# Row selection moved to ScalarE, and four more turns of the rank blocks moved to VectorE

## The chip, the cores and the metric

The kernel runs on one core of a Trainium2 chip. The metric is the device time of one execution in microseconds. Three executions of the kernel before took 880.44, 880.70 and 880.80 us (median 880.7).

## The reference, cut to what matters

Two layers are applied to 4096 tokens of width 1024, and each adds its result to its input.

```python
x = x + _L0_ffn_ref(_L0_cond_ref(x, ...), W_base, b_base, W_router, A, B)
x = x + _L1_ffn_ref(_L1_cond_ref(x, weight, bias, lora_a_weights, lora_b_weights,
                                 scaling_factors, adapter_id), base_W, router_W, lora_A, lora_B)
# L0_ffn: router logits, top 2 of 8 experts, softmax over the two, rank 16 per expert
logits = xf @ W_router.T
rw, sel = jax.lax.top_k(logits, TOP_K)
rw = jax.nn.softmax(rw, axis=-1)
h = jnp.einsum('td,erd->ter', xf, A)
lora = jnp.einsum('ter,te,eor->to', h, w, B) * SCALING
# L1_cond: one of 8 adapters of rank 16 for every sequence of 64 tokens
a_sel = lora_a_weights[adapter_id]
b_sel = lora_b_weights[adapter_id]
low = jnp.einsum('bsi,bri->bsr', x, a_sel)
delta = jnp.einsum('bsr,bor->bso', low, b_sel)
# L1_ffn: router, top 2 of 8, rank 16 per expert, as in L0_ffn
```

The kernel multiplies the weights of both layers together once (about the first 350 us). What is left for each token is one large product with the combined matrix, the router logits, and three low-rank parts: the rank block `m0` (8 experts x 16 = 128 columns) of the first layer, the adapter's low rank `low` of the second, and the rank block `mid` of the second layer.

## The kernel before, in words

After the weights, 16 tiles of 256 tokens are worked through (tiles 0 to 15, `tau`). Tiles 0 and 1 use plain products (`plain_products`, 96 matmuls of 128x512 each), tiles 2 to 15 a Winograd scheme with fewer matmuls (`winograd_products`). Every fp32 factor is split into a high part, written by ScalarE (`hi_of`, L1143), and a low part, written by VectorE (`lo_of`, L1516); a product is three matmuls.

The engines each run an own list, written out by hand, and meet at semaphores. For a tile the small chain is this, in order of data:

- TensorE: `x_product(tau)` multiplies the tile by `gx`, which holds the logits' and ranks' columns and, at two places for each block `b` of 128 tokens, the 16 columns of the adapter that the sequence has chosen. TensorE waits for `gsel_ok` there.
- VectorE: `front(tau)` (`route`, L1962 to L1985) takes the top two experts, and L1994 multiplies the ranks by their weights: `m0`. In the middle it needs an exponential from ScalarE (`rex`, L1398).
- `m0` is turned (tokens to ranks) into bank `TR`: in tiles 0 and 1 by TensorE, with two 128x128 transposes (`turn`, L856); from tile 2 on by VectorE (`m0_turn`, L2039), with 16 block transposes of 32x64.
- ScalarE: `m0_high`; VectorE: `m0_low`; TensorE: step x1 of `chain(tau, i)` (L871 to L873), which adds the turned `m0` times its columns. `i` counts the matmuls of the tile, and the table `CHAIN` says at which `i` TensorE stops for a step of the chain: (turn of m0, x1, mid) by tile.
- VectorE: `low_rank` (L2008, needs `gx`'s partner `bls`), `low_low`; TensorE: step mid of the chain (L884); VectorE: `back(tau)`, the second routing, whose product L2031 is `mid`.
- `mid` is turned: in tiles 0, 1, 2 and 15 by TensorE (`mid_turn`), in tiles 3 to 14 by VectorE. `mid_high`, `mid_low`; then the rank products of TensorE (L1114 to L1116 in tiles 0 and 1, L923 later).

Who chooses the adapter's columns: GpSimd. Its loop waits for `c_mm` and `lraw_s` of the tile before, loads an index from memory to a register four times (`value_load`), and after each copies 16 elements into `bls` (L577) and 18x16 into `gx` (L578). Only then does it wait for `c2_mm` and issue the tile's `p1sel` DMAs (L566).

Between these steps VectorE and ScalarE make the other factors: in tiles 0 and 1 the sums and splits `t2_raw`, `t4_raw`, `t1_raw` (L2069 to L2083) and `t_high`/`t_low`, whose results SyncE stores and loads again; the split of the next tile (`x_high`, `x_low`); and the copies of the four output banks (`out_copy`, L1423), which free a bank for the next tile (`ev[j]`). TensorE begins a tile's bank 0 after `ev[0]`. In Winograd tiles VectorE adds partial results (`out_parts`, L2162), and TensorE waits for the first of these sums, `x6_ok`, before it uses bank 4 again; and for `u3_part` (L2171) before the last low term.

Of the kernel before, what the change touches and what calls it, by code (L numbers as in the profile page):

```python
# [14 lines left out]
P = 128  # L15
# [4 lines left out]
E = 8  # L20
# [14 lines left out]
KH = KC // 2  # L35
CHAIN = [(30, 44, 76), (13, 24, 56), (None, 29, 46), (None, 29, 46)]
R7, R6, R4, R2, R3, R5, NR = 1, 2, 3, 4, 5, 6, 6
# [34 lines left out]
def build(nc, xq, wall, m1t, aallt, x0t, b0t, lb1, lorabt, loraa, wq, cbook, ids, packed, out,  # L72
          e_dram, p1_dram, b_dram, t_dram):
    with ExitStack() as ctx:
# [439 lines left out]
        def _(pool):  # L514
# [54 lines left out]
            for tau in range(NT2):  # L569
                if tau:  # L570
                    pool.wait_ge(c_mm, tau)
                    pool.wait_ge(lraw_s, tau)
                for b, c0 in enumerate((0, WX)):
                    for s in range(2):
                        n = tau * 4 + 2 * b + s
                        i = bass.ds(pool.value_load(idc[0:1, n:n + 1], min_val=0, max_val=E - 1), 1)
                        nc.gpsimd.tensor_copy(bls[:, b, s, :], bl[:, i, :].squeeze(1))  # L577
                        ins = nc.gpsimd.tensor_copy(gx[:, :, c0 + RK * s:c0 + RK * s + RK], gl[:, i, :, :].squeeze(1))  # L578
                ins.then_inc(gsel_ok, 1)
                if tau:  # L580
                    pool.wait_ge(c2_mm, tau)
                else:
                    pool.wait_ge(gsel_ok, 1)
                    pool.wait_ge(g_mm, M_ALL)
                    nc.gpsimd.memset(f(lowt[96:KL, :]), 1.0).then_inc(pz_ok, 1)
                    pool.wait_ge(pz_ok, 1)
                    nc.gpsimd.memset(f(lowt[96:96 + RK, :]), 0.0).then_inc(pz_ok, 1)
                    pool.wait_ge(pz_ok, 2)
                    for b in range(2):
                        nc.gpsimd.memset(f(p1sel[b][32:64, :]), 0.0).then_inc(pz_ok, 1)  # L590
                    pool.wait_ge(pz_ok, 4)
                load_p1(tau, ld_p1s, slice(D, NM1))
                if tau:
                    pool.wait_ge(low_mm, tau)
                load_p1(tau, ld_p1w, slice(0, D))
# [3 lines left out]
        def _(pe):  # L599
# [240 lines left out]
            def x_product(tau, halves=(0, 1)):  # L840

                u, last = tau if tau < REG else 0, KH * halves[-1] + KH
                pe.wait_ge(x_hi_s, 2 * tau + halves[-1] + 1)
                pe.wait_ge(x_lo_s, 2 * tau + halves[-1] + 1)
                pe.wait_ge(gsel_ok, tau + 1)
                for b in range(2):
                    cs, ts = slice(SX * b, SX * b + WX), slice(b * P, b * P + P)
                    for c in range(KH * halves[0], last):
                        mm = split_product(xb[:, b, cs], x_hi[u][:, c, ts], x_lo[u][:, c, ts],
                                           gx[:, c, cs], gx[:, 9 + c, cs], c == 0, c == KC - 1)  # L850
                if last == KC:
                    mm.then_inc(xx_mm, 1)

            def turn(v, n0):
                for b in range(2):
                    mm = nc.tensor.transpose(TR[:, n0 + b * P:n0 + b * P + P], v[:, b, :], ident)  # L856
                return mm

            def chain(tau, i):
                at_m0, at_x1, at_mid = CHAIN[min(tau, REG) + (tau + 1 == NT2)]  # L860
                if i == at_m0:
                    pe.wait_ge(m0_s, tau + 1)
                    turn(m0, 0).then_inc(t0_mm, 1)
                if i == at_x1:
# [23 lines left out]
            def mid_turn(tau):  # L888
                pe.wait_ge(mid_s, tau + 1)
                turn(midv, 0).then_inc(t2_mm, 1)  # L890

# [34 lines left out]
            def winograd_products(tau):  # L926
# [74 lines left out]

                if n:
                    pe.wait_ge(mid_s, tau + 1)
                else:
                    mid_turn(tau)
                x_product(tau + 1, (0,))
# [113 lines left out]
            low_terms(0, (0, 2, 1, 3))  # L1120
            mid_turn(0)
            x_product(1)
# [17 lines left out]
        def _(act):  # L1140
# [135 lines left out]
            hi_of(brow[0][0:1, 512:D], bk[6][0:1, :]).then_inc(brow_hi, 1)  # L1276

            def x_hi_part(tau, k):
                cs = slice(KH * k, KH * k + KH)
# [67 lines left out]
            x_hi_part(0, 0).then_inc(x_hi_s, 1)  # L1347
            x_hi_part(0, 1).then_inc(x_hi_s, 1)
            act.wait_ge(eb_lo_s, 14)
            for q in range(4):  # L1350
# [83 lines left out]
            x_high(1, 1)  # L1434
            t_high(1)
            rex(0, 1)
            mid_high(0)
            t_high(2)
            for j in (3, 0, 2, 1):
                out_copy(0, j)  # L1440
            rex(1, 0)
            x_high(2, 0)
            m0_high(1)
            x_high(2, 1)
            low_stack(1)
            t_high(3)
            rex(1, 1)
            mid_high(1)
            s_high(2, 1)
# [10 lines left out]
            for tau in range(REG, NT2):  # L1460
# [18 lines left out]
                if tau + 1 < NT2:  # L1479
                    x_high(tau + 1, 0)  # L1480
                rex(tau, 1)
                if tau + 1 < NT2:
                    x_high(tau + 1, 1)
                mid_high(tau)
# [20 lines left out]
        def _(v):  # L1505
# [494 lines left out]
            def low_rank(tau):  # L2000
                v.wait_ge(c_mm, tau + 1)
                v.wait_ge(gsel_ok, tau + 1)
                twice = lambda a: a.unsqueeze(1).to_broadcast([64, 2, RK])
# [38 lines left out]
            def m0_turn(tau):  # L2042
                v.wait_ge(m0_s, tau + 1)
                turn(m0).then_inc(t0_mm, 1)

# [30 lines left out]

            def t1_raw(h, between=None):
                r, (h12, l12), (h11, l11) = t_begin(3, h), g_part(h, 0, 1), g_part(h, 0, 0)
                link(nc.vector.tensor_tensor(r, h12, h11, ALU.subtract))
                if between:  # L2080
                    between()
                link(nc.vector.tensor_tensor(r, r, l12, ALU.add))
                nc.vector.tensor_tensor(r, r, l11, ALU.subtract).then_inc(t_raw_s, 1)  # L2083

            def t_low(n):
                for h in range(2):
                    cs = slice(2 * h, 2 * h + 2)
# [99 lines left out]

            v.wait_ge(gsel_ok, 1)
            link(nc.vector.memset(shares[:], 1.0))
            front(0)  # L2190
            v.wait_ge(af_hi_s, 4)
            lo_of(lb1_lo[:], lb1_raw[:], lb1_hi[:]).then_inc(af_lo_s, 1)
            v.wait_ge(af_lo_s, 4)
            t_low(0)
            m0_low(0)
            t2_raw(0)
# [5 lines left out]
            t_low(1)  # L2202
            back(0)
            t4_raw(0)
            t4_raw(1)
            mid_low(0)
            t_low(2)
            front(1)
            x_low(2, 0)
            m0_low(1)  # L2210
            x_low(2, 1)
            t1_raw(0, lambda: low_rank(1))
            low_low(1)
            t1_raw(1)
# [10 lines left out]
            for tau in range(REG, NT2):  # L2225
# [26 lines left out]
                back(tau, lambda: s3_low(tau))  # L2252
                if n and tau + 1 < NT2:
                    mid_turn(tau)
# [98 lines left out]
```

## Time and profile before

| | us |
|---|---|
| median of three executions | 880.7 |
| the profiled execution | 881.12 |
| its span | 878.9 |
| TensorE busy | 873.8 |
| VectorE busy | 768.1 |
| ScalarE busy | 325.8 |
| GpSimd busy | 157.1 |

The span is the part of the execution in which instructions run, 2.2 us less than its time. The granted clock of TensorE is full in all slices of the span but the last. Busy time of TensorE counts overlapping matmuls once. Times in rows are microseconds from the span's start. Tile 0 begins at 345 us, tile 1's large products at 388, tile 2's at 425; from tile 3 on a tile takes 32.6 us.

### The profile page before, as it was taken

The page shows a single profiled execution, that of the slowest core. Times are in us where ns is not written, and L with a number is a line of the kernel's source. Part 1 is how long each engine was busy: PE and PEld are TensorE (multiplying, and loading weights), DVE is VectorE, ACT ScalarE, POOL GpSimd, SP SyncE. Part 2 cuts the span into 40 slices and gives each one's busy share as a digit, 9 for nine tenths or more (in the row PEclk, how much of TensorE's full clock was granted, in tenths as well). Part 3 has the DMA queues.
Part 4 walks back from the last instruction along what each step waited for, and adds up shares of the span by engine and source line. Part 5 has one row for each costly group of instructions (what it writes and reads, how often), then busy time and mean ns, then how long its engine had stood idle before and what let it go on. Part 6 is the DMA issues. An engine that isn't in the chain of part 4 may idle for free.

```text
span 878.9 us, 13788 instructions
## 1 busy us (share of the span) xinstructions
PE 873.8 (99%) x4506; PEld 766.8 (87%) x4506; DVE 768.1 (87%) x1846; ACT 325.8 (37%) x525; POOL 157.1 (18%) x310
## 2 busy tenths in 40 slices
PE   9999999999999999999999999999999999999998
PEld 8999998888998888888888888888888888888887
DVE  6899999787787968878889999999999999999995
ACT  6589788421424434232322222222223223222221
POOL 0210020111001001412212312312312312302310
PEclk9999999999999999999999999999999999999999
DMA  9623440685412042484887987987887988887976
GB/s 346 224 93 118 126 138 25 212 273 177 143 49 96 1 144 75 152 312 174 251 273 265 313 291 256 307 298 257 301 294 256 307 277 275 305 287 257 314 253 224
DMA packets 62610, 191.93 MB, mean 218 GB/s; under 512 B 8256, under 2 KB 12742, under 8 KB 60620
## 3 DMA queue, kind: packets, MB, share of 16 engines
q1 hardware_dynamic: 50282, 158.92, 51.6%
q0 software_dynamic: 11968, 31.88, 12.8%
q8 instruction: 36, 0.59, 0.3%
q10 hardware_dynamic: 290, 0.26, 0.1%
q14 instruction: 34, 0.28, 0.1%
HBM read 158.80 MB, written 32.76 MB: 218 GB/s over the span
## 4 chain that ended last, share of the span: by engine, by line
PE 97%; DMA 2%; ACT 0%; DVE 0%; SPq 0%; issue 0%; DVEq 0%
PE bank L941 16%; PE bank L603 15%; PE bank L604 15%; PE bank L605 15%; PE bank L965 9%; PE bank L923 7%; PE bank L909 5%; PE bank L969 4%; PE bank L640 2%; PE bank L918 2%; PE bank L1066 2%; PE bank L747 2%; DMA t_lo<-t_scratch 1%; PE bank L647 1%; DMA m_raw<-m1t 0%; PE bank L618 0%
## 5 line engine op out<-in xcount | busy, mean ns | idle before, releaser
L941 PE MATMUL bank<-g_hi,xs 128*128 128x512 f32 x440 | 140.1, 390 | 0.0
L566 POOL DMA_DIRECT2D p1sel<-p_scratch x128 | 65.6, 512 | 263.6 <-issue 263.4
L2039 DVE STREAM_TRANSPOSE bank<-ranks_raw 32x64 f32<-32x64 f32 x416 | 106.5, 256 | 6.2
L941 PEld LDWEIGHTS bank<-g_hi,xs 128*128 128x128 f32 x440 | 82.6, 188 | 17.1
L965 PE MATMUL bank<-t_hi,xs 128*128 128x512 f32 x336 | 91.1, 393 | 0.0
L941 PE MATMUL bank<-g_lo,xs 128*128 128x512 f32 x220 | 86.5, 393 | 0.0
L603 PE MATMUL bank<-gx,xs 128*128 128x304 f32 x256 | 77.6, 303 | 0.0
L605 PE MATMUL bank<-gx,xs 128*128 128x304 f32 x256 | 77.4, 303 | 0.0
L604 PE MATMUL bank<-gx,xs 128*128 128x304 f32 x256 | 77.1, 301 | 0.0
L965 PEld LDWEIGHTS bank<-t_hi,xs 128*128 128x128 f32 x336 | 63.0, 188 | 14.3 <-DMA t_hi<-t_scratch 0.2
L1516 DVE TENSOR_TENSOR xs<-x_raw,xs 128x1024 fp32r<-128x1024 f32 x60 | 73.6, 1249 | 2.1 <-ACT xs L1143 1.2
L1143 ACT ACTIVATE xs<-x_raw 128x1024 fp32r<-128x1024 f32 x60 | 61.6, 1050 | 25.5 <-PE bank L969 24.7
L577 POOL COPY bls<-bl 128x16 f32 x64 | 33.9, 529 | 170.1 <-issue 84.9
L1695 DVE SCALAR_TENSOR_TENSOR rbuf<-qbuf,thr,rbuf 128x1024 f32<-128x1024 f32 x48 | 59.5, 1281 | 3.5 <-ACT rbuf L1202 3.0
L1202 ACT ACTIVATE rbuf<-rbuf,step 128x1024 f32<-128x1024 f32 x48 | 53.8, 1148 | 9.3 <-DVE rbuf L1689 6.2
L604 PE MATMUL bank<-m_lo,w_hi 128*128 128x388 f32 (+1 forms) x168 | 56.9, 338 | 0.0
L603 PE MATMUL bank<-m_hi,w_hi 128*128 128x388 f32 (+1 forms) x168 | 56.9, 338 | 0.0
L605 PE MATMUL bank<-m_hi,w_lo 128*128 128x388 f32 (+1 forms) x168 | 56.8, 338 | 0.0
L969 PE MATMUL bank<-t_lo,xs 128*128 128x512 f32 x168 | 51.9, 390 | 0.1
L605 PE MATMUL bank<-weff_hi,w_lo 128*128 128x512 f32 x128 | 49.8, 389 | 0.0
L604 PE MATMUL bank<-weff_lo,w_hi 128*128 128x512 f32 x128 | 49.8, 389 | 0.0
L603 PE MATMUL bank<-weff_hi,w_hi 128*128 128x512 f32 x128 | 49.8, 389 | 0.0
(390 smaller groups left out, 2122.3 us busy)
## 6 DMA issues: line engine op xcount, KB each, us to landing
t_hi<-t_scratch SPq DMA_DIRECT2D x82, 512.0 KB, 5.7
t_lo<-t_scratch SPq DMA_DIRECT2D x82, 512.0 KB, 6.7
x_raw<-xq SPq DMA_DIRECT2D x16, 1024.0 KB, 6.8
out<-ost SPq DMA_DIRECT2D x63, 256.0 KB, 6.6
p1sel<-p_scratch POOLq DMA_DIRECT2D x64, 192.0 KB, 6.0
w_raw<-wall SPq DMA_DIRECT2D x15, 512.0 KB, 4.8
w<-e_scratch SPq DMA_DIRECT2D x6, 1024.0 KB, 5.2
ea<-e_scratch POOLq DMA_DIRECT2D x8, 644.0 KB, 5.3
```

Of the source, the lines that this page charges most:

```text
L566: pool.dma_start(f(p1sel[b][64 * s:64 * s + STK, cs]), p1_dram[bass.ds(i * STK, STK), cs]).then_inc(sems[b], 16)
L603: nc.tensor.matmul(out_ap, lhs_hi, rhs_hi, start=first, stop=False, skip_group_check=True)
L604: nc.tensor.matmul(out_ap, lhs_hi, rhs_lo, start=False, stop=False, skip_group_check=True)
L605: return nc.tensor.matmul(out_ap, lhs_lo, rhs_hi, start=False, stop=last, skip_group_check=True)
L923: mm = nc.tensor.matmul(dst, l, m, start=first and k == 0, stop=k == 2, skip_group_check=True)
L941: mm = nc.tensor.matmul(bk[j][:], l[:, c, :], m[:, c, :], start=first and c + k == 0, stop=c + k == KH + 1, skip_group_check=True)
L965: nc.tensor.matmul(bk[j][:], x[u][:, c, :], t_hi[:, c, :], start=first and c + u == 0, stop=False, skip_group_check=True)
L969: mm = nc.tensor.matmul(bk[j][:], x[0][:, c, :], t_lo[:, c, :], start=False, stop=c == KH - 1, skip_group_check=True)
L1143: return nc.scalar.activation(dst, src, ACT.Identity)
L1516: return nc.vector.tensor_tensor(dst, src, f(hi), ALU.subtract)
L1695: nc.vector.scalar_tensor_tensor(rbuf[u][:], qbuf[u][:], thr[:, m:m + 1], rbuf[u][:], ALU.is_gt, ALU.mult).then_inc(r_ready[u], 1)
L2039: ins = nc.vector.transpose(turned[ks, :, ts], ranked[ts, :, ks])
```

## The change

ScalarE copies the adapter's columns (`select`), in two halves for each tile, each with its own place in ScalarE's list; `gsel_ok` now counts two for each tile, and who waits for it waits for both. GpSimd keeps only the DMAs. VectorE now turns `m0` of tiles 0 and 1 and `mid` of tiles 0 and 2, with its 16 block transposes, and TensorE keeps the turn of `mid` in tiles 1 and 15. The lists of VectorE and ScalarE in tiles 0 and 1 are put in another order around this, and `CHAIN` loses its first column and has other places for x1 and mid: x1 of tile 0 goes from matmul 44 to 39, x1 of tile 1 from 24 to 28, mid of tile 1 from 56 to 57.

```diff
-CHAIN = [(30, 44, 76), (13, 24, 56), (None, 29, 46), (None, 29, 46)]
+CHAIN = [(39, 76), (28, 57), (29, 46), (29, 46)]
...                                                    # GpSimd
             for tau in range(NT2):
                 if tau:
-                    pool.wait_ge(c_mm, tau)
-                    pool.wait_ge(lraw_s, tau)
-                for b, c0 in enumerate((0, WX)):
-                    for s in range(2):
-                        n = tau * 4 + 2 * b + s
-                        i = bass.ds(pool.value_load(idc[0:1, n:n + 1], min_val=0, max_val=E - 1), 1)
-                        nc.gpsimd.tensor_copy(bls[:, b, s, :], bl[:, i, :].squeeze(1))
-                        ins = nc.gpsimd.tensor_copy(gx[:, :, c0 + RK * s:c0 + RK * s + RK], gl[:, i, :, :].squeeze(1))
-                ins.then_inc(gsel_ok, 1)
-                if tau:
                     pool.wait_ge(c2_mm, tau)
...                                                    # TensorE, x_product
-                pe.wait_ge(gsel_ok, tau + 1)
+                pe.wait_ge(gsel_ok, 2 * tau + 2)
...                                                    # TensorE, chain
-                if i == at_m0:
-                    pe.wait_ge(m0_s, tau + 1)
-                    turn(m0, 0).then_inc(t0_mm, 1)
...                                                    # TensorE, tile 2 (n == 0) and tile 0
-                if n:
-                    pe.wait_ge(mid_s, tau + 1)
-                else:
-                    mid_turn(tau)
+                pe.wait_ge(mid_s, tau + 1)
...
-            mid_turn(0)
+            pe.wait_ge(mid_s, 1)
             x_product(1)
...                                                    # ScalarE
+            def select(tau, b):
+                c0 = WX * b
+                if tau:
+                    act.wait_ge(c_mm, tau)
+                    act.wait_ge(lraw_s, tau)
...
+                for s in range(2):
+                    n = tau * 4 + 2 * b + s
+                    i = bass.ds(act.value_load(idc[0:1, n:n + 1], min_val=0, max_val=E - 1), 1)
+                    nc.scalar.activation(bls[:, b, s, :], bl[:, i, :].squeeze(1), ACT.Identity)
+                    ins = nc.scalar.activation(gx[:, :, c0 + RK * s:c0 + RK * s + RK], f(gl[:, i, :, :].squeeze(1)),
+                                               ACT.Identity)
+                ins.then_inc(gsel_ok, 1)
...                                                    # ScalarE, before the tiles
             x_hi_part(0, 1).then_inc(x_hi_s, 1)
+            select(0, 0)
+            select(0, 1)
...                                                    # ScalarE, tiles 0 and 1
             t_high(1)
+            select(1, 0)
             rex(0, 1)
+            select(1, 1)
             mid_high(0)
             t_high(2)
-            for j in (3, 0, 2, 1):
+            for j in (3, 0):
                 out_copy(0, j)
             rex(1, 0)
+            for j in (2, 1):
+                out_copy(0, j)
             x_high(2, 0)
...                                                    # ScalarE, tiles 2 to 15
                     x_high(tau + 1, 0)
+                    select(tau + 1, 0)
                 rex(tau, 1)
                 if tau + 1 < NT2:
+                    select(tau + 1, 1)
                     x_high(tau + 1, 1)
...                                                    # VectorE
             front(0)
+            m0_turn(0)
...
+            m0_low(0)
             t_low(0)
-            m0_low(0)
             t2_raw(0)
...
             back(0)
+            mid_turn(0)
             t4_raw(0)
+            mid_low(0)
             t4_raw(1)
-            mid_low(0)
-            t_low(2)
+            t_low(2, (0,))
             front(1)
+            m0_turn(1)
+            m0_low(1)
+            t_low(2, (1,))
+            low_rank(1)
             x_low(2, 0)
-            m0_low(1)
+            low_low(1)
             x_low(2, 1)
-            t1_raw(0, lambda: low_rank(1))
-            low_low(1)
+            t1_raw(0)
             t1_raw(1)
...
-                if n and tau + 1 < NT2:
+                if tau + 1 < NT2:
                     mid_turn(tau)
```

VectorE's list in tile 0, from the product of the second routing (`ranks_raw<-bank,gate`, which is `mid`) to the first routing of tile 1 (`MAX`). Before:

```order
L2031 TENSOR_TENSOR ranks_raw<-bank,gate 128x256
L2074 TENSOR_TENSOR t_raw<-g_hi,t_raw 128x1024
L2075 TENSOR_TENSOR t_raw<-t_raw,g_lo 128x1024
L2074 TENSOR_TENSOR t_raw<-g_hi,t_raw 128x1024
L2075 TENSOR_TENSOR t_raw<-t_raw,g_lo 128x1024
L1516 TENSOR_TENSOR midt_lo<-bank,midt_hi 128x256
L1516 TENSOR_TENSOR t_lo<-t_raw,t_hi 128x1024 x2
L1962 MAX best<-bank 128x8
```

The same place of the changed kernel:

```order
L2038 TENSOR_TENSOR ranks_raw<-bank,gate 128x256
L2046 STREAM_TRANSPOSE bank<-ranks_raw 32x2x32 x16
L2083 TENSOR_TENSOR t_raw<-g_hi,t_raw 128x1024
L2084 TENSOR_TENSOR t_raw<-t_raw,g_lo 128x1024
L1523 TENSOR_TENSOR midt_lo<-bank,midt_hi 128x256
L2083 TENSOR_TENSOR t_raw<-g_hi,t_raw 128x1024
L2084 TENSOR_TENSOR t_raw<-t_raw,g_lo 128x1024
L1523 TENSOR_TENSOR t_lo<-t_raw,t_hi 128x1024
L1969 MAX best<-bank 128x8
```

The 16 block transposes and `mid_low` now stand ahead of the second half of `t4_raw`, and one of the two instructions of `t_low(2)` has gone behind the routing.

ScalarE's list over the same time, from `mid_high(0)` to the first split of tile 2. Names `ost_84`, `ost_81`, `ost_83`, `ost_82` are the output copies of banks 3, 0, 2, 1. Before:

```order
L1143 ACTIVATE midt_hi<-bank 128x256
L1143 ACTIVATE t_hi<-t_raw 128x1024 x2
L1423 ACTIVATE ost_84<-bank 128x512
L1423 ACTIVATE ost_81<-bank 128x512
L1423 ACTIVATE ost_83<-bank 128x512
L1423 ACTIVATE ost_82<-bank 128x512
L1398 ACTIVATE shares<-shares 128x2
L1143 ACTIVATE xs<-x_raw 128x4x256
```

The changed kernel, from the last index of `select(1, 1)` on:

```order
L1269 TENSOR_LOAD idc
L1269 ISA x2
L1270 ISA
L1270 ACTIVATE bls<-bl 128x16
L1271 ISA
L1271 ACTIVATE gx<-gl 128x18x16
L1123 ACTIVATE midt_hi<-bank 128x256
L1123 ACTIVATE t_hi<-t_raw 128x1024 x2
L1422 ACTIVATE ost_84<-bank 128x512
L1422 ACTIVATE ost_81<-bank 128x512
L1397 ACTIVATE shares<-shares 128x2
L1422 ACTIVATE ost_83<-bank 128x512
```

The exponential of tile 1's first routing now comes after two output copies, not four; the output copies still stand behind both halves of `t_hi`.

## Rows read from the trace of the kernel before

**Rows 1.** The page, busy time of each engine.
```profile
PE 873.8 (99%) x4506; PEld 766.8 (87%) x4506; DVE 768.1 (87%) x1846; ACT 325.8 (37%) x525; POOL 157.1 (18%) x310
```

**Rows 2.** TensorE's longest wait in the span: engine, line, releaser: us, times, longest.
```profile
PE bank L629 <- DVE warm L1560: 1.1, 1, 1.1
```

**Rows 3.** Timeline of TensorE, m0's turn in tile 0: start, duration, instruction.
```profile
358.65 0.38 PE L856 MATMUL bank<-pk,ranks_raw 128*128 128x128 f32 x2
358.79 0.48 PE L909 MATMUL bank<-g_hi,xs 128*128 128x512 f32 x1
359.10 0.40 PE L909 MATMUL bank<-g_lo,xs 128*128 128x512 f32 x1
```

**Rows 4.** Timeline of VectorE, m0's turn in blocks in tile 2.
```profile
424.48 0.42 DVE L1994 TENSOR_TENSOR ranks_raw<-bank,gate 128x256 f32<-128x256 f32 x1
424.94 4.30 DVE L2039 STREAM_TRANSPOSE bank<-ranks_raw 32x64 f32<-32x64 f32 x16
429.69 0.42 DVE L1516 TENSOR_TENSOR m0t_lo<-bank,m0t_hi 128x256 fp32r<-128x256 f32 x1 [0.45 <-ACT m0t_hi L1143]
```

**Rows 5.** Timeline of VectorE, tile 0; in brackets idle time before, and its releaser.
```profile
359.49 0.42 DVE L1516 TENSOR_TENSOR m0t_lo<-bank,m0t_hi 128x256 fp32r<-128x256 f32 x1 [1.59 <-ACT m0t_hi L1143]
...
362.98 0.59 DVE L2008 TENSOR_TENSOR lraw<-bank,bls 64x32 f32<-64x32 f32 x4 [0.68 <-PE bank L873]
...
379.20 1.23 DVE L2075 TENSOR_TENSOR t_raw<-t_raw,g_lo 128x1024 f32<-128x1024 f32 x1
```

**Rows 6.** Timeline of TensorE: mid's turn of tile 0, and tile 1's first large product.
```profile
378.60 0.38 PE L856 MATMUL bank<-pk,ranks_raw 128*128 128x128 f32 x2
...
388.26 0.39 PE L909 MATMUL bank<-g_hi,xs 128*128 128x512 f32 x1
```

**Rows 7.** Timeline of ScalarE: the output copies, then a split and an exponential in tile 3.
```profile
386.40 2.65 ACT L1423 ACTIVATE ost<-bank 128x512 f32<-128x512 f32 x4 [2.94 <-PE bank L1116]
...
467.40 1.05 ACT L1143 ACTIVATE xs<-x_raw 128x1024 fp32r<-128x1024 f32 x1
471.20 0.20 ACT L1398 ACTIVATE shares<-shares 128x2 f32<-128x2 f32 x1 [2.75 <-DVE shares L1965]
```

**Rows 8.** Timeline of VectorE, tile 1.
```profile
385.71 0.18 DVE L1962 MAX8 best<-bank 128x8 f32<-128x8 f32 x1 [0.98 <-PE bank L605]
...
389.18 0.17 DVE L1977 TENSOR_SCALAR rs<-shares 128x2 f32<-128x2 f32 x1 [2.30 <-ACT shares L1398]
...
392.05 0.42 DVE L1516 TENSOR_TENSOR m0t_lo<-bank,m0t_hi 128x256 fp32r<-128x256 f32 x1 [0.61 <-ACT m0t_hi L1143]
...
415.88 0.42 DVE L1516 TENSOR_TENSOR midt_lo<-bank,midt_hi 128x256 fp32r<-128x256 f32 x1 [1.55 <-ACT midt_hi L1143]
...
422.15 0.17 DVE L1962 MAX8 best<-bank 128x8 f32<-128x8 f32 x1 [0.18 <-PE bank L605]
```

**Rows 9.** Timeline of VectorE, tile 2 and the start of tile 3.
```profile
432.16 0.59 DVE L2008 TENSOR_TENSOR lraw<-bank,bls 64x32 f32<-64x32 f32 x4 [0.72 <-PE bank L873]
...
436.33 1.47 DVE L1516 TENSOR_TENSOR xs<-x_raw,xs 128x1024 fp32r<-128x1024 f32 x1
...
450.64 0.69 DVE L2171 TENSOR_TENSOR p_sum<-bank,p_sum 128x512 f32<-128x512 f32 x1 [1.73 <-PE bank L923]
...
453.98 0.17 DVE L1962 MAX8 best<-bank 128x8 f32<-128x8 f32 x1 [0.39 <-PE bank L605]
...
463.14 0.42 DVE L1516 TENSOR_TENSOR m0t_lo<-bank,m0t_hi 128x256 fp32r<-128x256 f32 x1
```

**Rows 10.** Timeline of TensorE, tile 3: step x1, and the product that needs the selection.
```profile
464.12 0.29 PE L871 MATMUL bank<-gx,m0t_hi 128*128 128x272 f32 x1
...
475.55 0.30 PE L603 MATMUL bank<-gx,xs 128*128 128x304 f32 x1
```

**Rows 11.** Timeline of GpSimd, tile 3: two of the four copies into bls.
```profile
466.38 0.20 POOL L577 COPY bls<-bl 128x16 f32 x1 [6.94 <-DVE lraw L2008]
...
467.17 0.58 POOL L577 COPY bls<-bl 128x16 f32 x1 [0.22 <-issue]
```

More of the change, by code:

```diff
@@ L570, in _ @@
                 if tau:
-                    pool.wait_ge(c_mm, tau)
-                    pool.wait_ge(lraw_s, tau)
-                for b, c0 in enumerate((0, WX)):
-                    for s in range(2):
-                        n = tau * 4 + 2 * b + s
-                        i = bass.ds(pool.value_load(idc[0:1, n:n + 1], min_val=0, max_val=E - 1), 1)
-                        nc.gpsimd.tensor_copy(bls[:, b, s, :], bl[:, i, :].squeeze(1))
-                        ins = nc.gpsimd.tensor_copy(gx[:, :, c0 + RK * s:c0 + RK * s + RK], gl[:, i, :, :].squeeze(1))
-                ins.then_inc(gsel_ok, 1)
-                if tau:
                     pool.wait_ge(c2_mm, tau)
                 else:
-                    pool.wait_ge(gsel_ok, 1)
                     pool.wait_ge(g_mm, M_ALL)
@@ L852, in x_product @@
                     mm.then_inc(xx_mm, 1)
[L854 to L857, printed above, removed]
             def chain(tau, i):
-                at_m0, at_x1, at_mid = CHAIN[min(tau, REG) + (tau + 1 == NT2)]
-                if i == at_m0:
-                    pe.wait_ge(m0_s, tau + 1)
-                    turn(m0, 0).then_inc(t0_mm, 1)
+                at_x1, at_mid = CHAIN[min(tau, REG) + (tau + 1 == NT2)]
                 if i == at_x1:
@@ L889, in mid_turn @@
                 pe.wait_ge(mid_s, tau + 1)
-                turn(midv, 0).then_inc(t2_mm, 1)
+                for b in range(2):
+                    mm = nc.tensor.transpose(TR[:, b * P:b * P + P], midv[:, b, :], ident)
+                mm.then_inc(t2_mm, 1)
             def plain_products(tau):
@@ L1276, in _ @@
             hi_of(brow[0][0:1, 512:D], bk[6][0:1, :]).then_inc(brow_hi, 1)
+            def select(tau, b):
[3 more added lines that the diff above has]
+                    act.wait_ge(lraw_s, tau)
+                elif not b:
+                    act.wait_ge(ids_ok, 2)
+                    act.wait_ge(g_lo_s, OC11)
+                    act.wait_ge(bias_ok, 1)
+                for s in range(2):
[5 more added lines that the diff above has]
+                ins.then_inc(gsel_ok, 1)
             def x_hi_part(tau, k):
@@ L1445, in _ @@
             low_stack(1)
+            select(2, 0)
             t_high(3)
             rex(1, 1)
+            select(2, 1)
             mid_high(1)
@@ L2001, in low_rank @@
                 v.wait_ge(c_mm, tau + 1)
-                v.wait_ge(gsel_ok, tau + 1)
+                v.wait_ge(gsel_ok, 2 * tau + 2)
                 twice = lambda a: a.unsqueeze(1).to_broadcast([64, 2, RK])
@@ L2043, in m0_turn @@
                 v.wait_ge(m0_s, tau + 1)
+                if not tau:
+                    v.wait_ge(g_lo_s, O_ALL)
                 turn(m0).then_inc(t0_mm, 1)
@@ L2075, in t4_raw, with t1_raw, t_low @@
                 nc.vector.tensor_tensor(r, r, l21, ALU.add).then_inc(t_raw_s, 1)
-            def t1_raw(h, between=None):
+            def t1_raw(h):
                 r, (h12, l12), (h11, l11) = t_begin(3, h), g_part(h, 0, 1), g_part(h, 0, 0)
                 link(nc.vector.tensor_tensor(r, h12, h11, ALU.subtract))
-                if between:
-                    between()
                 link(nc.vector.tensor_tensor(r, r, l12, ALU.add))
                 nc.vector.tensor_tensor(r, r, l11, ALU.subtract).then_inc(t_raw_s, 1)
-            def t_low(n):
-                for h in range(2):
+            def t_low(n, parts=(0, 1)):
+                for h in parts:
                     cs = slice(2 * h, 2 * h + 2)
@@ L2186, in out_lower_right @@
                 out_sum(tau, 3, bk[4], p1_sum)
-            v.wait_ge(gsel_ok, 1)
+            v.wait_ge(gsel_ok, 2)
             link(nc.vector.memset(shares[:], 1.0))
             front(0)
+            m0_turn(0)
             v.wait_ge(af_hi_s, 4)
```

## The prediction, made before the changed kernel had run

> **What bounds the kernel now.** I read the page first: TensorE is busy 873.8 of 878.9 us, VectorE 768.1, ScalarE 325.8, GpSimd 157.1 [rows 1]. Then TensorE's waits: the longest is 1.1 us, at the very start [rows 2], and nothing in the tiles names VectorE or ScalarE. So TensorE is the bound, and time can be won only by taking work from it. Last I read the timelines of the first tiles, because the change works there, and ask of every step how long before TensorE's need it is done. The answer is: seldom more than 1 us. The profiled execution took 881.12 us, its span 878.9; the median of the runs is 0.42 lower, 880.7. I add to 881.12 and take the 0.42 off at the end.
>
> **What TensorE is relieved of.** A pair of transposes starts at 358.65, where the next large matmul would have started. The second large matmul after that point starts at 359.10 [rows 3]; two large matmuls in a row start 0.23 apart (358.65 to 358.88), so a pair delays TensorE by 0.22. Four pairs go (m0 and mid of tile 0, m0 of tile 1, mid of tile 2): 4 x 0.22 = 0.88 us. Those of tiles 1 (mid) and 15 stay. That is all the gain TensorE can show: 881.12 - 0.88 = 880.24 if nothing is late.
>
> **What VectorE is given.** A turn in blocks takes 4.30 and begins 0.46 after the product before it (424.48 to 424.94), where an instruction that needs nothing would have begun after some 0.35: 4.4 us each, four times 17.6. A split that follows a turn directly also waits 0.45 for ScalarE [rows 4]. A rule of the Trainium skill speaks against such a move (VectorE: DVE Perf Modes, Rules for kernel authors): transpose 128x128 with TensorE if the result may go to PSUM, as it does here. By the trace the rule's prices are 0.22 against 4.30 us. By busy time alone the move would be worth its 0.88 us; by the rule it is bad wherever VectorE is what TensorE waits for next. So I follow VectorE through three places.
>
> **First place: the output bank that tile 1 begins with.** Before, VectorE ended `t4_raw(1)` at 379.20 + 1.23 = 380.43. Added ahead of that: two turns, 8.8, and `mid_low`, 0.4. What this fills: the waits of 1.59 and 0.68 in tile 0 [rows 5], and about 0.5 that the copies of GpSimd cost VectorE and that end (a split which takes 1.23 elsewhere took 1.47 beside them in tile 2 [rows 9]; I take twice the difference for a tile, an estimate). 380.43 + 9.2 - 2.77 = 386.9. Then ScalarE has the second half of `t_hi` (1.05, by the like split of rows 7) and two output copies (2.65 / 4 = 0.66 each, and a little less as no matmul holds them back): `ev[0]` at 389.0 to 389.2. TensorE would be there at 388.26 [rows 6] less two pairs, 387.8. So a wait of about 1.2 us, and more than the whole gain is gone. Before, the copies ended at 389.05 all four, and bank 0's was long done [rows 7]; now `t_hi`'s second half comes before them. Step x1 of tile 0 (matmul 39, nine matmuls of 0.23 after 358.65, 360.7) is just met: adding VectorE's list from its first routing gives `m0t_lo` at 360.4.
>
> **Second place: step x1 of tile 1 and the start of tile 2.** The routing of tile 1 begins at 386.9 + 1.1 = 388.0, 2.3 later than 385.71. To the routing of tile 2: + 4.4 + 0.45 (turn and its split), + 1.2 (the other half of `t_low(2)`); filled are waits of 2.30, 0.61 and 1.55, and two more of about half a us each, like the 0.61 [rows 8]; GpSimd gives back 0.5 to 0.8. VectorE was ready for tile 2 at 421.97. 421.97 + 2.3 + 6.05 - 4.46 - 1.0 - 0.65 = 424.2; adding the instructions of this stretch in their new order by their spacing gives 423.6, so 1.4 to 2.0 late. TensorE meets x1 of tile 1 about when m0t_lo is ready (395.4), so it waits at most 0.2 there, and in tile 2 it had 1.2 us to spare at x1 (m0t_lo done at 430.1 [rows 4]; `low_rank`, which starts some 0.9 after x1 does, at 432.16 [rows 9]); VectorE is late by 1.4 or more, TensorE itself by 0.5: no wait, or one of a few tenths.
>
> **Third place: step x1 of tile 3.** Before, `m0t_lo` was done at 463.14 + 0.42 = 463.56 and TensorE took it at 464.12 [rows 9, 10]. Now VectorE comes 1.5 late, has mid's turn (4.4), and can fill 0.72, 1.73 and 0.39 [rows 9] and 0.5 from GpSimd: 463.56 + 1.5 + 4.4 - 2.84 - 0.5 = 466.1. On the way TensorE waits twice, for `u3_part` (about 0.1) and for `x6_ok`, the first sum of `out_parts`, some 1.0. Whatever was waited for before is part of this one: TensorE's x1 goes from 464.12 to 466.1 or 466.2. **The sum is +2.0 us**: 0.88 won, 2.9 waited (about 1.2 at `ev[0]`, 0.1 at x1 of tile 1, 1.1 in tile 2's end, 0.5 at x1 of tile 3). From tile 3 on VectorE does what it did, without GpSimd's copies beside it, and TensorE's own pace returns. 881.12 + 2.0 = 883.1; less 0.42: 882.7.
>
> **The selection on ScalarE.** GpSimd came to its next index after 0.79 us (466.38 to 467.17) while the copies went on [rows 11]. On ScalarE no row shows a load of an index. Low end: the same 0.79, so a half of two indices takes 1.6 and the last copy 0.4: 2.0. High end: the load not hidden behind the two copies, which by 0.20 for 2 elements and 1.05 for 1024 [rows 7] take 0.2 and 0.45: 1.43 an index, 2.9 a half. In tile 3 ScalarE is free from 468.4 to 471.2 and again from 471.4 until TensorE needs the columns at 475.55 [rows 7, 10]: 2.8 and 4.1. For tile 1 the second half begins behind the exponential, at about 375.5 by VectorE's new list, and TensorE comes at 378.60 - 0.22 [rows 6]: 2.9. Both ends fit; I take nothing. If a half took over 3.5, the two halves and the exponential would pass 475.55 in each of 13 tiles. The Trainium skill gives a floor of about 600 ns for a tensor_load (DMA: Bandwidth & Descriptors, Latency and other measured facts); by it an index would cost some 0.3 more than GpSimd's, an estimate, still inside the high end. The DMAs of GpSimd come 1 to 2 us sooner, as they no longer stand behind the copies; nobody waits for them, so nothing.
>
> **Rivals.**
> A, the forecast: VectorE is late by its turns, +2.0, own range +0.8 to +3.4. For it: VectorE has 2.8 us of idle time in tile 2 to set against 4.4, and three hand-overs with under 1 us to spare.
> B, not slower: the turns are hidden, because VectorE gains more from the end of GpSimd's copies and from the new order than I count. It must be 2.9 us earlier at x1 of tile 3 for the full gain, 2.0 for no change: 880.7 - 0.9 = 879.8 in full, up to 880.7 + 0.8 in part. For it: all three places are sums of many short terms, and each was off by a few tenths when I added it in two ways. Against it: 17.6 us of turns, and the idle spans named at the three places add up to 10.6 (2.27 + 4.46 + 1.0 + 2.84).
> C, the selection: a half takes 3.5 + h us on ScalarE and TensorE waits 2h in each of 13 tiles; with h of 0.2 that is 5 us, 887. Against it: the bounds above. It decides from 3.5 on.
> D, VectorE doesn't recover: the lateness of tile 3 returns at x1 in later tiles, as it had only 0.5 to spare; 0.3 in each of 5 tiles, 884.5.
>
> **How the numbers follow.** A 0.60, B 0.24, C 0.07, D 0.09. The predicted time is A's, 882.7. The range 880.0 to 885.0 leaves out the full B's lower part, C, and the far end of D, and holds about 8 in 10. 0.2% is 1.76 us and about what a measurement here can tell: slower than 882.46 are six tenths of A, C and D: 0.52. Same is the rest of A and most of B: 0.43. Faster than 878.9 would need twice what the four pairs cost: 0.05.
>
> **What the profile would show.** Right: TensorE has waits that name ScalarE's output copy L1422 at about 388 (1 us), VectorE's L2169 (`out_parts`) at about 457 (1 us) and `m0t_lo` at about 465; VectorE has 480 block transposes of bank, not 416; its splits beside the old copies fall from 1.47 to 1.23; from tile 4 on no waits. Wrong: no TensorE wait between 350 and 470 (B), or waits on `gx` in each tile with ScalarE's L1271 as releaser (C), or at x1 in tile after tile (D).

## The result and the profile after

The changed kernel took 881.77 us (median of 22 executions, 881.62 to 882.88), the kernel before 880.72 beside it (22 executions, 880.12 to 882.27). The ratio is 1.0013, 95% interval 1.0007 to 1.0019: slower by 1.05 us, which is less than the 0.2% named as what counts. The forecast was 882.7, range 880.0 to 885.0. The profiled execution took 882.67, its span 881.0 us.

The page's busy times, to set against [rows 1]:

```profile
PE 874.2 (99%) x4498; PEld 766.5 (87%) x4498; DVE 773.9 (88%) x1910; ACT 358.9 (41%) x653; POOL 96.5 (11%) x182
```

The four pairs of transposes are gone (8 matmuls fewer), yet TensorE is not less busy. VectorE has 5.8 us more, less than the 17.6 that it was given. Three groups of the view by line show the most of why, first of the changed kernel, then of the kernel before (line, form, count | busy us, mean ns):

```profile
L2046 DVE STREAM_TRANSPOSE bank<-ranks_raw 32x64 f32<-32x64 f32 x480 | 122.9, 256 | 7.2
L1523 DVE TENSOR_TENSOR xs<-x_raw,xs 128x1024 fp32r<-128x1024 f32 x60 | 72.0, 1222 | 2.5 <-ACT xs L1123 2.1
L1523 DVE TENSOR_TENSOR lowt<-lowr,lowt 16x128 fp32r<-16x128 f32 x32 | 9.0, 283 | 1.3 <-ACT lowt L1123 0.6
```

```profile
L2039 DVE STREAM_TRANSPOSE bank<-ranks_raw 32x64 f32<-32x64 f32 x416 | 106.5, 256 | 6.2
L1516 DVE TENSOR_TENSOR xs<-x_raw,xs 128x1024 fp32r<-128x1024 f32 x60 | 73.6, 1249 | 2.1 <-ACT xs L1143 1.2
L1516 DVE TENSOR_TENSOR lowt<-lowr,lowt 16x128 fp32r<-16x128 f32 x32 | 14.7, 460 | 1.3 <-ACT lowt L1143 0.6
```

64 more block transposes, 16.4 us, as expected. The splits of the tiles, whose mean was 1249 ns beside GpSimd's copies, are at 1222 without them, 1.6 us less in all. The larger part comes from the small subtraction in `low_low`: 32 instructions, 5.7 us less.

TensorE's waits of 0.2 us or more (line, releaser: us, times, longest). Of these, before had only the first [rows 2]:

```profile
PE bank L592 <- ACT gx L1271: 1.4, 1, 1.4
PE bank L618 <- DVE warm L1567: 1.1, 1, 1.1
PE bank L906 <- DVE p_sum L2169: 0.6, 1, 0.6
PE bank L852 <- DVE m0t_lo L1523: 0.2, 1, 0.2
PE bank L952 <- DMA t_lo<-t_scratch: 0.2, 1, 0.2
```

The view counts a wait from the modelled end of the matmul before. What TensorE loses is read better from the starts, which are 0.23 apart for two 128x512 matmuls. TensorE's timeline at the three places:

```profile
378.15 0.40 PE L1046 MATMUL bank<-p1sel,lowt 114*128 114x512 f32 x1
379.93 0.38 PE L592 MATMUL bank<-gx,xs 128*128 128x304 f32 x1 [1.38 <-ACT gx L1271]
...
457.24 0.39 PE L906 MATMUL bank<-lb_hi,srk_lo 128*128 128x512 f32 x1
458.23 0.50 PE L906 MATMUL bank<-k_hi,srk_hi 128*128 128x512 f32 x1 [0.61 <-DVE p_sum L2169]
458.57 0.39 PE L906 MATMUL bank<-k_lo,srk_hi 128*128 128x512 f32 x1
...
465.38 0.39 PE L924 MATMUL bank<-g_lo,xs 128*128 128x512 f32 x1
465.95 0.36 PE L852 MATMUL bank<-gx,m0t_hi 128*128 128x272 f32 x1 [0.18 <-DVE m0t_lo L1523]
```

Ahead of tile 1 it loses 1.78 - 0.23 = 1.55 us, at `x6_ok` 0.99 - 0.23 and another 0.10 (0.34 to the next start), 0.9 in all, and at x1 of tile 3 0.57 - 0.23 and a tenth behind it, 0.4. With 0.88 won that is 2.0, and x1 of tile 3 starts at 465.95, 1.83 after that of before [rows 10]. There was no wait at the output bank of tile 1. In its place stands the one that the prediction had set at nothing, for the columns that ScalarE chooses. ScalarE's timeline there:

```profile
375.38 0.20 ACT L1397 ACTIVATE shares<-shares 128x2 f32<-128x2 f32 x1 [3.03 <-DVE shares L1972]
377.53 0.22 ACT L1270 ACTIVATE bls<-bl 128x16 f32 x1 [1.95 <-issue]
377.65 0.43 ACT L1271 ACTIVATE gx<-gl 128x288 fp32r x1
379.24 0.22 ACT L1270 ACTIVATE bls<-bl 128x16 f32 x1 [1.16 <-issue]
379.36 0.43 ACT L1271 ACTIVATE gx<-gl 128x288 fp32r x1
```

"issue" means that the engine waited for no semaphore: it was loading the index. The instructions of that line, over the whole span and then from 370 to 374 us (durations in ns, min/median/max):

```profile
L1269 ACTq TENSOR_LOAD <-idc x64: 272/277/1741, 323.4 to 832.8; - x64
...
L1269 ACTq TENSOR_LOAD <-idc x2: 275/278/282, 370.4 to 371.2; - x2
```

The longest of them, 1.74 us, begins at 375.44, as soon as the exponential has started.

GpSimd has index loads too, one for each `p1sel` DMA (L565). In the trace of the kernel before, where ScalarE loads no index, three of them fall in this stretch and take about 1 us or more, against a median of 289 ns:

```profile
L565 POOLq TENSOR_LOAD <-idc x3: 996/1217/1503, 373.1 to 378.8; - x3
```

So the sign of a slow stretch stood in the trace that the prediction was made from.

### The profile page after: what moved, and what is told of

It reads as the page before. It is cut to its first block, busy times and chain, and to the rows that moved or that the text cites. A ratio compares the mean times of both kernels' runs of the same rounds, so it can differ in the third digit from the quotient of the medians.

```text
span 881.0 us, 13856 instructions
## 1 busy us (share of the span) xinstructions
PE 874.2 (99%) x4498; PEld 766.5 (87%) x4498; DVE 773.9 (88%) x1910; ACT 358.9 (41%) x653; POOL 96.5 (11%) x182
## 4 chain that ended last, share of the span: by engine, by line
PE 90%; DVE 6%; DMA 2%; issue 1%; ACT 0%; ACTq 0%; SPq 0%; DVEq 0%
PE bank L924 15%; PE bank L592 15%; PE bank L594 15%; PE bank L593 15%; PE bank L948 8%; PE bank L906 6%; PE bank L952 4%; PE bank L892 2%; PE bank L629 2%; PE bank L736 2%; PE bank L1046 1%; DMA t_lo<-t_scratch 1%; DVE bank L2046 1%; PE bank L901 1%; PE bank L636 1%; DVE xs L1523 1%
## 5 line engine op out<-in xcount | busy, mean ns | idle before, releaser
L2046 DVE STREAM_TRANSPOSE bank<-ranks_raw 32x64 f32<-32x64 f32 x480 | 122.9, 256 | 7.2
L1523 DVE TENSOR_TENSOR xs<-x_raw,xs 128x1024 fp32r<-128x1024 f32 x60 | 72.0, 1222 | 2.5 <-ACT xs L1123 2.1
L592 PEld LDWEIGHTS bank<-gx,xs 128*128 128x128 f32 x256 | 48.2, 188 | 2.9 <-issue 1.8
```

The source lines that it names most:

```text
L592: nc.tensor.matmul(out_ap, lhs_hi, rhs_hi, start=first, stop=False, skip_group_check=True)
L1523: return nc.vector.tensor_tensor(dst, src, f(hi), ALU.subtract)
L2046: ins = nc.vector.transpose(turned[ks, :, ts], ranked[ts, :, ks])
```

## Experiments

Theory V: VectorE's list up to x1 of tile 3 decides the time, and the wait for `gx` lies beside it. Theory S: the wait for `gx` is the loss.

**The selection back on GpSimd.** On GpSimd the loop of the kernel before, with `ins.then_inc(gsel_ok, 2)`; on ScalarE:

```diff
-            select(1, 0)
             rex(0, 1)
-            select(1, 1)
...
-                    select(tau + 1, 0)
                 rex(tau, 1)
...
```

> The changed kernel with one part undone: GpSimd chooses the columns again, as before; the four turns stay on VectorE and every list else is that of the changed kernel. Theory V (VectorE's list up to step x1 of tile 3 sets the time, and TensorE's wait of 1.5 us for gx in front of tile 1 lies beside it): the wait for gx goes, a wait for the output copy of bank 0 of about 1.2 us takes its place at 388, VectorE's splits beside GpSimd's copies take some 1.4 us instead of 1.23 and x1 of tile 3 comes 0.3 to 1.0 us later than in the changed kernel: 882.0 to 882.8 us, against 881.8 of the changed kernel. Theory S (the wait for gx is the loss): it goes and nothing takes its place, 880.2 us.

Measured: 884.49 us (5 executions, from 883.93; ratio 1.0042, 1.0028 to 1.0056). Theory S has fallen, and theory V's size was too small. The page's busy times, then TensorE's waits from 345 us on:

```profile
PE 874.7 (99%) x4498; PEld 766.2 (87%) x4498; DVE 783.4 (89%) x1910; ACT 324.9 (37%) x525; POOL 159.3 (18%) x310
```

```profile
PE bank L903 <- ACT ost L1414: 1.4, 1, 1.4
PE bank L917 <- DVE p_sum L2155: 0.6, 1, 0.6
PE bank L959 <- ACT ost L1414: 0.4, 1, 0.4
PE bank L1057 <- DVE p_sum L2164: 0.3, 1, 0.3
```

The predicted wait for the output copy has appeared (L903, 1.4), and a second at the start of tile 2 (L959). VectorE is busy 9.5 us longer than in the changed kernel (783.4): GpSimd's copies cost it 0.6 us in each of 16 tiles. Three tiles of that are 1.8, and x1 of tile 3 is later by 1.9:

```profile
467.86 0.37 PE L863 MATMUL bank<-gx,m0t_hi 128*128 128x272 f32 x1
```

So without the move of the selection the turns would cost 2.7 us more by the medians, 1.9 of them seen in the trace up to tile 3: the move makes room for a part of the turns. The profiled execution took 883.94; the other 0.5 us of the median was not followed.

**The selection alone.** The kernel before, with `select` on ScalarE at the changed kernel's places:

```diff
             t_high(1)
+            select(1, 0)
             rex(0, 1)
+            select(1, 1)
```

> The kernel before with the other part alone: ScalarE chooses the columns, at the same places of its list as in the changed kernel; all turns and the table CHAIN are those of the kernel before. Both theories expect no loss from tile 2 on. In front of tile 1 TensorE needs gx at 378.9 us: if the two index loads of the second half take 1.2 to 1.7 us each as in the changed kernel, a wait of about 1 us appears there, and since TensorE bounds the kernel before and nothing else waits, theory S expects the whole of it in the time: 881.5 to 882.0. Theory V says the same of the wait if it appears, but VectorE is ready earlier in every tile. If the slow loads were a chance of one execution: 880.7.

Measured twice, 880.16 us (11 executions; ratio 0.9994, 0.9984 to 1.0003), and

> The kernel before with the selection alone on ScalarE once more, as its interval reached from -0.16% to +0.03%. If its TensorE has no wait at all, it lies at the low end of the kernel before: 880.1 to 880.2 us, and 0.5 us under its median. If that was chance: 880.7.

880.12 (11; 0.9998, 0.9989 to 1.0007). The slow loads were there again (1.27 us each, at 373.4 and 375.2), but the exponential comes earlier in this kernel, so the columns were chosen at 377.3, before TensorE came for them. TensorE's waits are one only, that of the first microseconds, and VectorE is busy 9.7 us less than in [rows 1]:

```profile
PE bank L618 <- DVE warm L1574: 1.1, 1, 1.1
```

```profile
PE 873.9 (99%) x4506; PEld 767.2 (87%) x4506; DVE 758.4 (86%) x1846; ACT 359.7 (41%) x653; POOL 96.8 (11%) x182
```

It costs nothing. Whether its median, 0.7 and 0.5 us under that of before beside it (880.9 and 880.66), is a gain stays open: both intervals hold 1. The lowest executions hardly differ (880.07 and 880.01 against 880.12 and 880.07); what differs is how many lie near the lowest. Counted from the start of tile 0, TensorE starts x1 of tiles 0 to 9 at the same time in both profiles, within 0.01 us; then before loses 0.55 us to one late load of `t_lo` at 668. Such a late load stands in the changed kernel's profile too, at 605, and not in this one's.

**The selection of tile 1 earlier.**

```diff
-            t_high(1)
             select(1, 0)
-            rex(0, 1)
+            t_high(1)
             select(1, 1)
+            rex(0, 1)
```

> The changed kernel with ScalarE's two halves of the selection for tile 1 some 3 us earlier: the first ahead of the split t_high(1), the second right behind it and ahead of the exponential. TensorE then has no wait for gx in front of tile 1. Theory V: it arrives at bank 0 of tile 1 at 387.8 us and waits there 1.0 to 1.2 us for ScalarE's output copy; x1 of tile 3 is still at 465.9 and the time is still 881.7 (within 0.3). Theory S: 1.5 us less, 880.3.

Measured: 881.66 us (ratio 1.0011, 1.0002 to 1.0020), 0.1 less than the changed kernel. Theory V holds, with the new wait where it said. TensorE's waits in the tiles, and x1 of tile 3 in its timeline:

```profile
PE bank L892 <- ACT ost L1422: 0.9, 1, 0.9
PE bank L906 <- DVE p_sum L2169: 0.6, 1, 0.6
PE bank L852 <- DVE m0t_lo L1523: 0.2, 1, 0.2
```

```profile
465.63 0.36 PE L852 MATMUL bank<-gx,m0t_hi 128*128 128x272 f32 x1 [0.15 <-DVE m0t_lo L1523]
```

A wait of 1.55 us taken away gave back 0.3 in the profile, since the next one took its place.

**The turn of `mid` of tile 2 back on TensorE.**

```diff
-                pe.wait_ge(mid_s, tau + 1)
+                if n:
+                    pe.wait_ge(mid_s, tau + 1)
+                else:
+                    mid_turn(tau)
...                                                    # VectorE
-                if tau + 1 < NT2:
+                if n and tau + 1 < NT2:
                     mid_turn(tau)
```

> The changed kernel with the turn of mid of tile 2 back on TensorE (a pair of transposes, 0.22 us) and out of VectorE's list (4.4 us); all else stays. Theory V: VectorE is 4.4 us earlier at x1 of tile 3, the waits of TensorE at 457 (0.87 us) and 465 (0.43 us) go, 0.22 comes back: 1.1 us less than the changed kernel, 880.7 us, the same as the kernel before. Theory S (tile 1 is where all is lost): 0.2 us more than the changed kernel, 882.0.

Measured: 880.77 us (ratio 1.0001, 0.9992 to 1.0011). The forecast to the tenth: this one turn of 4.3 us on VectorE cost the changed kernel 1.0 us, by the medians all that it lost. By the trace a part is left: x1 of tile 3 is still 0.6 us later than in [rows 10]. Both waits of tile 2's end are gone; in the tiles only that for `gx` is left, and x1 of tile 3 is 1.24 us earlier than in the changed kernel:

```profile
PE bank L592 <- ACT gx L1274: 0.9, 1, 0.9
```

```profile
464.71 0.29 PE L852 MATMUL bank<-gx,m0t_hi 128*128 128x272 f32 x1
```

**All named waits taken away, three turns kept.** Both edits above, and:

```diff
-CHAIN = [(39, 76), (28, 57), (29, 46), (29, 46)]
+CHAIN = [(39, 76), (32, 57), (29, 46), (29, 46)]
...
-            t_high(2)
+            t_high(2, (0,))
             for j in (3, 0):
                 out_copy(0, j)
+            t_high(2, (1,))
             rex(1, 0)
```

> All that the changed kernel's waits named is taken away at once, and three of the four turns stay on VectorE: the selection of tile 1 early, the turn of mid of tile 2 on TensorE, ScalarE's output copies of banks 3 and 0 ahead of the second half of t_hi, and x1 of tile 1 at matmul 32, not 28. Theory V (VectorE's list has no cover for three turns): TensorE reaches x1 of tile 2 at 430.7 us, 0.7 earlier than before, but VectorE has m0t_lo only at 431.4, as in the two runs with a wait taken away; the 0.66 us of the three pairs is given back there, and the time is that of the selection alone, 880.2 us. Rival W (only the waits named so far cost anything): 880.1 - 0.66 = 879.5 us.

Measured: 880.60 us (ratio 1.0000, 0.9991 to 1.0009). Rival W has fallen. Theory V gave the direction, but not the place or quite the size: TensorE waits 0.4 at x1 of tile 1 (by starts) and 0.7 for the output copy at the start of tile 2, not at x1 of tile 2. Three pairs won, 0.66, and 1.1 waited make 0.44 more than the selection alone; the medians differ by 0.46:

```profile
PE bank L948 <- ACT ost L1425: 0.4, 1, 0.4
PE bank L852 <- DVE m0t_lo L1527: 0.2, 1, 0.2
```

**Only the turns of `m0` of tiles 0 and 1, with the early selection.** Both turns of `mid` are TensorE's again, tile 2's as above and tile 0's by:

```diff
-            pe.wait_ge(mid_s, 1)
+            mid_turn(0)
             x_product(1)
...                                                    # VectorE
             back(0)
-            mid_turn(0)
```

> The changed kernel with both turns of mid (tiles 0 and 2) back on TensorE, so that VectorE has only those of m0 of tiles 0 and 1, 8.8 us, and with the selection of tile 1 early. Theory V: VectorE is 4.4 us earlier in tile 1 than in the changed kernel and nothing waits; two pairs stay won, 0.44 us less than the kernel with the selection alone (880.1): 879.7 us, faster than both. Rival R (a turn on VectorE never gains, since VectorE is late somewhere): 880.1 or more.

Measured: 879.58 us (ratio 0.9986, 0.9977 to 0.9995), and once more

> The kernel with the two turns of m0 alone on VectorE and the early selection once more, beside the selection alone. Two pairs of transposes at 0.22 us less on TensorE and no wait: 0.44 to 0.55 us under the kernel with the selection alone, 879.6 us.

879.86 (0.9989, 0.9980 to 0.9998): faster than both kernels, by 0.1% against before. Over both runs of each, 22 executions, it is 879.70 against 880.14 of the selection alone: 0.44, the two pairs (0.58 in the first runs of each, 0.26 in the second). From the start of tile 0 to the end of the span the profiles have 532.71 and 532.75 us against 533.23 and 533.25, 0.5 less. TensorE has the one wait of the first microseconds only, and x1 of tile 3 is half a microsecond before [rows 10]:

```profile
463.62 0.29 PE L852 MATMUL bank<-gx,m0t_hi 128*128 128x272 f32 x1
```

**The same two turns, with the selection where the changed kernel has it.**

> As the kernel with the two turns of m0 alone on VectorE, but with the selection of tile 1 where the changed kernel has it, its second half behind the exponential, in the 8 us in which an index load of ScalarE took 1.2 to 1.9 us. Theory V says that this wait was hidden in the changed kernel only because VectorE was later; here nothing is, so TensorE's wait for gx in front of tile 1 (0.6 to 1.2 us) stands in the time in full: 880.3 to 880.9 us. If it costs nothing here either: 879.7, as with the early selection.

Measured: 880.74 us (ratio 0.9999, 0.9990 to 1.0008): 1.04 us more than the 879.70 of the early selection. The wait that cost 0.1 us in the changed kernel costs 1.0 where VectorE has time to spare. TensorE's wait, and ScalarE's two index loads:

```profile
PE bank L592 <- ACT gx L1274: 0.8, 1, 0.8
```

```profile
L1272 ACTq TENSOR_LOAD <-idc x2: 1188/1312/1435, 375.7 to 377.4; - x2
```

**The two index loads moved, the copies not.**

```diff
             select(1, 0)
+            ids = index(6), index(7)
             rex(0, 1)
-            select(1, 1)
+            select(1, 1, ids)
```

> The kernel with the two turns of m0 alone on VectorE and the late selection of tile 1 (measured 880.74), with one edit: the two index loads of the second half stand right behind the first half, at about 372.5 us, where the DMA engines are busy 0.22 of the time, and the registers are kept over the exponential; the four copies stay behind it. Theory L (the slow index loads, 1.2 to 1.9 us each in a stretch with the DMA engines busy 0.88 to 0.94, make the wait for gx): the loads take 0.3 us, the copies are done 1 us behind the exponential, the wait goes, 879.6 us. Rival K (it is the copies, or whatever else ScalarE does there): the wait of 1.2 us stays, 880.7 us.

Measured: 879.64 us (ratio 0.9987, 0.9978 to 0.9996). Theory L holds: all four loads between 371.3 and 373.3 take 0.28, and the copies of the second half follow the exponential at once.

```profile
L1262 ACTq TENSOR_LOAD <-idc x4: 275/276/283, 371.3 to 373.3; - x4
```

```profile
376.22 0.20 ACT L1403 ACTIVATE shares<-shares 128x2 f32<-128x2 f32 x1 [3.02 <-DVE shares L1979]
376.38 0.22 ACT L1276 ACTIVATE bls<-bl 128x16 f32 x1
376.50 0.43 ACT L1277 ACTIVATE gx<-gl 128x288 fp32r x1
```

## Why the prediction was right, and where it was not

- **TensorE's gain, 0.88 us for four pairs: right in size.** Two pairs left out with nothing to wait for are worth 0.44 by the pooled medians and 0.5 by the profiles (the m0 turns against the selection alone). The changed kernel won all of it and lost more.
- **A turn costs VectorE 4.4 us: right.** VectorE's timeline at the two turns that the sum followed longest:

```profile
377.20 4.30 DVE L2046 STREAM_TRANSPOSE bank<-ranks_raw 32x64 f32<-32x64 f32 x16
...
387.80 0.17 DVE L1969 MAX8 best<-bank 128x8 f32<-128x8 f32 x1
...
423.51 0.17 DVE L1969 MAX8 best<-bank 128x8 f32<-128x8 f32 x1
...
460.45 4.30 DVE L2046 STREAM_TRANSPOSE bank<-ranks_raw 32x64 f32<-32x64 f32 x16
...
465.39 0.41 DVE L1523 TENSOR_TENSOR m0t_lo<-bank,m0t_hi 128x256 fp32r<-128x256 f32 x1
```

 Tile 1's routing was forecast at 388.0 and began at 387.80, tile 2's at 423.6 to 424.2 and began at 423.51. `m0t_lo` of tile 3, forecast at 466.1, was done at 465.80. What counted was to follow one engine's list through three tiles, with its idle spans as credit.
- **GpSimd's share in VectorE's time, 0.5 us a tile: right in size, but partly by luck.** The two runs with the selection exchanged give 9.5 and 9.7 us over 16 tiles, 0.6. The forecast took it from one split of 1.47 us in tile 2, which did fall to 1.23. Over all tiles these splits give back 1.6 us in all, 0.1 a tile; `low_low`, which the prediction did not name, gives 5.7.
- **The first place, 1.2 us at `ev[0]`: it did not occur in the changed kernel.** TensorE was late already. It did occur as soon as the other wait was taken away (0.9 in that view, 388.83 - 387.57 - 0.23 = 1.0 by the starts), and with the selection on GpSimd.
- **The step that failed: "Both ends fit; I take nothing" for the selection.** The high end for a half was 2.9 us, which was all the time there was, and one took 4.4 (375.4 to 379.8). The price of an index was taken from GpSimd's in tile 3, where it is quick, and used for ScalarE's in tile 1; the kernel before had slow loads of GpSimd in just that stretch. The sum came out all the same because the wait for `gx` took the place of that at `ev[0]`, as the early selection showed; rival C's place was right and its size wrong, since only tile 1 was hit, not 13 tiles.
- **Tile 2's end and x1 of tile 3, 1.1 and 0.5: right, 0.9 and 0.4.** Giving that one turn back to TensorE removed both.
- **No waits from tile 4 on: right, but for the one late `t_lo` load.** Rival D has fallen. Rival B, that the turns are hidden, is true of the two m0 turns and false of the two mid turns.
- **The size.** The forecast was +2.0 against 880.7 and the medians give +1.05. The trace is nearer to the forecast: +1.8 at x1 of tile 3. From the start of tile 0 to the end of the span it is +1.9, if the late `t_lo` load that each of the two profiles has is left out (0.55 us in before, 0.69 in the changed kernel). One part of this is not that of most executions: the slowest index load, 1.74 us against 1.2 to 1.4 in the four other profiles with that load late. The kernel with the early selection, whose profile has neither a slow index load in this place nor a late `t_lo`, took 881.65 in its profiled execution. The other part is the spread of the kernel before. The lowest executions of the two kernels are 1.50 us apart; the median of before lies 0.60 above its lowest, that of the changed kernel 0.15. In each set of executions with the selection on GpSimd the median is 0.56 to 0.79 above the lowest, in each with it on ScalarE 0.04 to 0.49. So some 0.5 us of the difference between forecast and result seems to be won by the move of the selection, which the prediction set at nothing. What spreads the executions, late loads of `t_lo` or other things, no row shows.
- **Two sums of rivals don't come out of their terms.** C's 2h in 13 tiles is 5.2 us, which gives 885.0 from the full gain of B, or 887.9 on top of A, not 887; D's five times 0.3 on top of A is 884.2, not 884.5. Neither rival was what happened.

## What to carry to other kernels

Work moved off the bounding engine is won only where the engine that takes it has idle time before the next hand-over: two of four turns had it, and were worth their 0.44 us; one of the others cost 1.0 us, more than four pairs of transposes are worth. When several waits stand in a row on one chain, taking away the first shows only that the second takes its place, so follow the late engine's list to the last of them and give back work there. And price an operation where it will stand, not where a quiet row shows it: another engine's loads in the same stretch had the price.

## What the runs showed of the hardware

An index load from on-chip memory to a ScalarE register takes 0.28 us in the median and up to 1.74 (64 loads). The slow pairs stood in one stretch in every kernel that had them there (1.74 and 1.24 us in the changed kernel, 1.2 to 1.4 each in the four other profiles with them there), in which the DMA engines are nearly full. Those of tile 1 for tile 2 are between, 0.62 to 0.91 us. The changed kernel by stretches (us, busy time of each engine, granted clock, DMA share, GB/s):

```profile
371.00:374.00 3.00, 3.00 (x15) 2.48 (x14) 3.00 (x4) 1.35 (x5) 1.18 (x3) 1.00 0.18 31
374.00:377.00 3.00, 3.00 (x15) 2.44 (x14) 2.80 (x16) 0.20 (x1) 0.85 (x2) 1.00 0.98 277
377.00:380.00 3.00, 1.62 (x8) 1.03 (x6) 2.83 (x12) 1.10 (x4) 0.00 (x0) 1.00 0.95 357
```

It is nothing of ScalarE's own: in every kernel at least one of GpSimd's index loads in this stretch took 0.96 us or more, also where ScalarE had none there (1.22, 1.50 and 1.00 us in the kernel before). That the traffic is the cause was not shown: moving the loads by some 4 us changed more than the DMA share, and in later tiles, with the DMA engines busy 0.8 of the time, most loads are quick (median 277 ns from 480 us on, the slowest 742). It is shown that moving them makes them quick. By the Trainium skill (DMA: Bandwidth & Descriptors, Latency and other measured facts) a tensor_load takes at least about 600 ns; here the floor is 272 ns, and the measurement decides.

GpSimd's copies slowed VectorE, which showed in full only when they were taken away. In the view by line of the kernel before they are busy for 64.9 us:

```profile
L577 POOL COPY bls<-bl 128x16 f32 x64 | 33.9, 529 | 170.1 <-issue 84.9 <-DVE lraw L2008 84.6
L578 POOL CAST gx<-gl 128x288 fp32r x64 | 31.0, 485 | 0.0
```

VectorE's busy time fell by 9.7 us without them, 0.15 us for each us of copies. The largest part, 5.7 us, is that of `low_low`, whose instructions of 16x128 elements took 460 ns in the mean and take 283 now; they follow `low_rank`, which is what GpSimd's copies waited for, and in tile 3 ran from 467.73 to 468.83 beside copies from 466.38 to 470.51. The Trainium skill (SBUF — State Buffer, SBUF: two separate sides) says that the two engines share a pair of ports by an exclusive lock, and that a VectorE operation with two inputs in SBUF can be the one that blocks or is blocked, against a GpSimd operation that reads SBUF. Both agree with it, the lengthened splits with the inputs `x_raw` and `xs` and `low_low` with `lowr` and `lowt`; no run here tells a lock from a shared bandwidth.
